# A gated attention layer with a mixture of experts: the residual's scaled normalisation split over VectorE, ScalarE and GpSimd

## Chip, core and metric

One core of a Trainium2 chip. The metric is the device time of one execution in microseconds. Start times in the text are from the profiled span's start.

## What is computed

The first half is an mLSTM attention on 8 sequences of 512 tokens and 256 features, 8 heads, and its output `h` is normalised per token and added to `x`. The second half routes every token to 2 of 9 experts. Cut to what matters:

```python
def _mlstm_cell(q, k, v, ...):                       # q = layernorm(x), k = v = ctx
    C = qk * D_mat                                   # per head, causal
    h = einsum('hst,htd->hsd', C / (normalizer + EPS), vh)
    mu = h.mean(axis=-1, keepdims=True)
    var = h.var(axis=-1, keepdims=True)
    return (h - mu) / sqrt(var + LN_EPS) * ln_scale
x = x + tanh(g_xattn[0]) * _mlstm_cell(...)
x = x + tanh(g_ffn[0]) * experts(layernorm(x))       # top 2 of 9, hidden 704
```

## The kernel before

The program is written by hand: each engine has its own list of instructions, in the order of the code, and semaphores between them. It has three parts. The first (to about 76 us) normalises `x`, transposes it and computes the gates. The second is the attention, in 32 **slots** `t`, one for each tile of 128 tokens (4 tiles `c = t % 4` to a sequence), to about 300 us. The third routes and runs the experts (line 1091 is their matmuls).

In the second part every engine runs one function per slot, `slot_pe`, `slot_act`, `slot_dve`, `slot_pool` and `slot_sync`, and each of them works on several tiles at once: while tile `t` gets its `h`, the decay matrix of tile `t+2` is prepared and tile `t-2` is normalised for the router.

- **VectorE** (`slot_dve`, order of the instructions in a slot): three small steps for the divisor (L620, L622, L624), `h` from PSUM (L627), its statistics (L648) and their mean and variance `mv` (L651), the same for the finished `x2` of tile `t-2` (L657, L660), the state (L610, two instructions; a copy, L605, for one tile in four, nothing for another), `Cm` of tile `t+2` (L587, two), `nb` = minus mean times 1/deviation (L670, 2 columns), and `Cl`, the low bf16 part of `Cm` (L595, two).
- **ScalarE** (`slot_act`): `x2 = h*rs + nb` of tile `t-1` (L677, `c_hn_act`), `y` of `t-3` (L685), the exponentials (L543), `vp` (L555), `yT` (L701), then `lv` and `rs` of tile `t` (L694, L696, `c_rs_act`), which wait for VectorE's L660. Then it waits for GpSimd's last `whl` of the slot before, issues its store (L470, `w_store`), rounds `Cm` to `Ch` (L549, two) and rounds a piece of the experts' weights to bf16 (L464, `w_hi_act`).
- **GpSimd** (`slot_pool`): `kw` (L568) and `qE` (L576), each for three tiles in four, `vp` (L560), then `c_pool` of tile `t-1`: `x2 = x2*lsg` (L712) and `x2 = x2 + xc` (L715), where `lsg` is `tanh(g)*ln_scale` in all partitions and `xc` the residual. Last comes the low part of the weights' piece, in three thirds of 408 columns (L479, `w_pool`), which waits for ScalarE's L464 (semaphore `w_hi`). Slots 0 to 29 have such a piece, slot 13 excepted.
- **TensorE** (`slot_pe`): the products with `Ch` and `Cl` of tile `t`, the scores of tile `t+2`, the decay of `t+3` (L509, L511), the router's products of `t-5` (L729) and a transpose (L721).

`Cm` and `Dm`, `Ch`, `Cl`, `h`, `x2`, `xc` and `lsg` lie in SBUF, `bank` is PSUM. `c_xn` counts ScalarE's finished `x2`, `c_x2` GpSimd's, `c_x2o` the stores to the output.

Of the kernel before, what the change touches and what calls it, by code (L numbers as in the profile page):

```python
# [20 lines left out]
ALU = mybir.AluOpType  # L21
ACT = mybir.ActivationFunctionType
# [10 lines left out]
NC = S // P  # L33
# [27 lines left out]
def build(nc, x, kv, wgate, fib, lnrow, gsc, wroute, rbias, wts, out):  # L61
    with ExitStack() as ctx:
        def sb(name, shape, dt=F32):
            return ctx.enter_context(nc.sbuf_tensor(name, shape, dt))

        def sem(name):
            return ctx.enter_context(nc.semaphore(name))
# [28 lines left out]
        h = sb("h", [P, NC, D])  # L96

        xc = [sb(f"xc{w}", [P, NC, D]) for w in range(2)]; st2 = sb("st2", [P, NC, 6]); st3 = sb("st3", [P, NC, 6])
        mv = sb("mv", [P, NC, 2, 2]); lv = sb("lv", [P, NC, 2]); rs = sb("rs", [P, NC, 2]); nb = sb("nb", [P, NC, 2])
        x2 = sb("x2", [P, NC, D]); y = sb("y", [P, NC, D])  # L100
# [64 lines left out]
        w_in = [sem(f"w_in{w}") for w in range(2)]; w_hi = sem("w_hi"); w_lo = sem("w_lo")  # L165
        w_out = [sem(f"w_out{w}") for w in range(2)]
        c_x = [sem(f"c_x{w}") for w in range(2)]; c_st2 = sem("c_st2"); c_mv2 = sem("c_mv2"); c_st3 = sem("c_st3"); c_mv3 = sem("c_mv3")
        c_nb = sem("c_nb"); c_lv = sem("c_lv"); c_rs = sem("c_rs"); c_xa = sem("c_xa"); c_xn = sem("c_xn"); c_x2 = sem("c_x2"); c_y = sem("c_y"); c_yT = sem("c_yT"); c_yc = sem("c_yc")
        c_lp = sem("c_lp"); c_lg = sem("c_lg"); c_x2o = [sem(f"c_x2o{c}") for c in range(NC)]; c_yo = [sem(f"c_yo{c}") for c in range(NC)]
        s_pace = sem("s_pace")  # L170

        def fence(eng):

            eng.sem_inc(s_pace, 1)

        def ge(eng, sem, val):


            if isinstance(val, int):
                if val > 0:  # L180
                    eng.wait_ge(sem, val)
                return
            eng.wait_ge(sem, val)
            if eng.engine in (nc.sync.engine, nc.gpsimd.engine):
                fence(eng)
# [394 lines left out]
        def b_c_dve(dve, t):  # L580
            for g in range(2):
                ge(dve, b_D, 2 * t + g + 1)
                ge(dve, b_s, t + 1)
                ge(dve, b_Ch, 2 * t + g - 3)
                ge(dve, b_Cl, 2 * t + g - 3)
                by4 = lambda a: a.rearrange("p (j s) -> p j s", j=HG)
                nc.vector.scalar_tensor_tensor(by4(Cm[t % 2][g][:, :]), bank[:, 4:8, g * P:(g + 1) * P], SCALE,  # L587
                                               by4(Dm[t % 2][g][:, :]), ALU.mult, ALU.mult).then_inc(b_C, 1)

        def b_cl_dve(dve, t):  # L590
            ge(dve, b_h, t - 1)
            for g in range(2):
                k = 2 * (t % 2) + g
                ge(dve, b_Ch, 2 * t + g + 1)
                nc.vector.tensor_tensor(Cl[k][:, :], Cm[t % 2][g][:, :], Ch[k][:, :], ALU.subtract).then_inc(b_Cl, 1)  # L595

        def b_st_dve(dve, t):
            V = nc.vector
            b, c = t // NC, t % NC
            if c < NC - 1:  # L600
                ge(dve, b_s, t + 2)
                ub = bank[:, 4:6, UO:UO + HG * DV]
                ge(dve, b_h, t)
                if c == 0:
                    V.tensor_copy(St[0][:, :, :], ub).then_inc(b_st, 1)  # L605
                else:
                    if t == 1:
                        ge(dve, s_dec, 16 * HG)
                    for g in range(2):
                        ins = V.scalar_tensor_tensor(St[c % 2][:, g, :], St[1 - c % 2][:, g, :], dec[:, b, g, c:c + 1],  # L610
                                                     ub[:, g, :], ALU.mult, ALU.add)
                    ins.then_inc(b_st, 1)

        def b_h_dve(dve, t):
            V = nc.vector
            c = t % NC
            ge(dve, b_h, t + 1)
            byg = lambda a: a.rearrange("p (g h) -> p g h", g=2)
            x = hp[:, :, :, DH]
            V.scalar_tensor_tensor(byg(n1[:, :]), x, N_EPS, byg(col[:, t, NH:2 * NH]), ALU.subtract, ALU.max, reverse0=True).then_inc(b_n, 1)  # L620
            ge(dve, b_n, t * 3 + 1)
            V.scalar_tensor_tensor(byg(n2[:, :]), x, N_EPS, byg(n1[:, :]), ALU.add, ALU.max).then_inc(b_n, 1)  # L622
            ge(dve, b_n, t * 3 + 2)
            V.reciprocal(n3[:, :], n2[:, :]).then_inc(b_n, 1)  # L624
            ge(dve, b_n, t * 3 + 3)
            ge(dve, c_xn, t - 3)
            V.tensor_tensor(h[:, c, :].rearrange("p (g h e) -> p g h e", g=2, e=DH), hp[:, :, :, 0:DH],  # L627
                            byg(n3[:, :]).unsqueeze(3).to_broadcast([P, 2, HG, DH]), ALU.mult).then_inc(b_ho, 1)
# [15 lines left out]
        def c_sth_dve(dve, t):  # L644
            V = nc.vector
            c = t % NC
            ge(dve, b_ho, t + 1)
            V.bn_stats(st2[:, c, :], h[:, c, :]).then_inc(c_st2, 1)  # L648
            ge(dve, c_st2, t + 1)
            ge(dve, c_xn, t - 3)  # L650
            V.bn_aggr(mv[:, c, 0, :], st2[:, c, :]).then_inc(c_mv2, 1)  # L651

        def c_stx_dve(dve, t):
            V = nc.vector
            c = t % NC
            ge(dve, c_x2, t + 1)
            V.bn_stats(st3[:, c, :], x2[:, c, :]).then_inc(c_st3, 1)  # L657
            ge(dve, c_st3, t + 1)
            ge(dve, c_y, t - 3)
            V.bn_aggr(mv[:, (c + 2) % NC, 1, :], st3[:, c, :]).then_inc(c_mv3, 1)  # L660

        def c_nb_dve(dve, t):
            r = t % NC
            lo, hi = (0 if t < NT else 1), (2 if t >= 2 else 1)
            ge(dve, c_rs, t + 1)
            ge(dve, c_mv2, min(t + 1, NT))
            ge(dve, c_mv3, t - 1)
            ge(dve, c_xn, t - 3)
            ge(dve, c_y, t - 5)
            nc.vector.scalar_tensor_tensor(nb[:, r, lo:hi], mv[:, r, lo:hi, 0], -1.0, rs[:, r, lo:hi], ALU.mult, ALU.mult).then_inc(c_nb, 1)  # L670

        def c_hn_act(act, t):
            c = t % NC
            ge(act, c_nb, t + 1)
            ge(act, c_y, t - 3)
            ge(act, c_x2o[c], 16 * (t // NC))
            nc.scalar.activation(x2[:, c, :], h[:, c, :], ACT.Identity, bias=nb[:, c, 0:1], scale=rs[:, c, 0:1]).then_inc(c_xn, 1)  # L677

        def c_y_act(act, t):
            c = t % NC  # L680
# [27 lines left out]
        def c_pool(pool, t):  # L708
            G = nc.gpsimd
            b, c = t // NC, t % NC  # L710
            ge(pool, c_xn, t + 1)
            G.tensor_tensor(x2[:, c, :], x2[:, c, :], lsg[:, :], ALU.mult).then_inc(c_xa, 1)  # L712
            ge(pool, c_xa, t + 1)
            ge(pool, c_x[b % 2], 16 * (b // 2) + 16)
            G.tensor_tensor(x2[:, c, :], x2[:, c, :], xc[b % 2][:, c, :], ALU.add).then_inc(c_x2, 1)  # L715

# [29 lines left out]
        def slot_act(act, t):  # L746
            if 0 <= t - 1 < NT:
                c_hn_act(act, t - 1)
            if 0 <= t - 3 < NT:
                c_y_act(act, t - 3)  # L750
            if 1 <= t + 2 < NT:
                b_exp_act(act, t + 2)
            if 1 <= t + 1 < NT:
                b_vh_act(act, t + 1)
            if 0 <= t - 5 < NT:
                c_yc_act(act, t - 5)
            if t >= 9 and (t - 9) % NC == 0:
                c_lg_act(act, (t - 9) // NC)
            if 0 <= t < NT + 2:
                c_rs_act(act, t)  # L760
            if t in PIECE:
                w_store(act, PIECE[t] - 1)
            if t - 1 in PIECE and PIECE[t - 1] == NT - 1:
                w_store(act, NT - 1)
            if 0 <= t + 2 < NT:
                b_ch_act(act, t + 2)
            if t in PIECE:
                w_hi_act(act, PIECE[t])

        def slot_dve(dve, t):  # L770
            if 0 <= t < NT:
                b_h_dve(dve, t)
            if 0 <= t < NT:
                c_sth_dve(dve, t)
            if 0 <= t - 2 < NT:
                c_stx_dve(dve, t - 2)
            if 0 <= t + 1 < NT - 1:
                b_st_dve(dve, t + 1)
            if 0 <= t + 2 < NT:
                b_c_dve(dve, t + 2)  # L780
            if 0 <= t < NT + 2:
                c_nb_dve(dve, t)
            if 0 <= t + 2 < NT:
                b_cl_dve(dve, t + 2)
# [648 lines left out]
```

## Time and profile before

| | |
|---|---|
| time, median of 3 runs | 779.48 us (778.26 to 780.39) |
| profiled execution | 777.09 us |
| its span | 775.3 us |
| PE busy | 663.8 us (86%) |
| DVE busy | 516.8 us (67%) |
| ACT busy | 386.7 us (50%) |
| POOL busy | 409.1 us (53%) |
| mean granted TensorE clock | 0.831 |

PE is TensorE, DVE VectorE, ACT ScalarE and POOL GpSimd. The span runs from the first instruction to the last; the execution's own time is 1.8 us more. The shares are means over three parts with different limits, so those of the second part are read from the trace by stretch. A clock of 1.0 is 2.4 GHz, 0.5 is 1.2 GHz. In a timeline two instructions of a pipelined engine overlap a little: the step from one start to the next is the time that an instruction costs. A row with x2 or x3 holds so many instructions that follow each other.

### The profile page before, as it was taken

To read this page: it belongs to the slowest core of one execution; us is meant where nothing else is said; L and a number is where in the kernel's file an instruction comes from. 1 tells how busy PE (TensorE), PEld (TensorE's weight loads), DVE (VectorE), ACT (ScalarE), POOL (GpSimd) and SP (SyncE) were. 2 spreads that over 40 slices of the span, in tenths; PEclk is the share of its full clock that TensorE was granted. 3 is DMA by queue.
4 is the path that set the end of the run, shared out by engine and by line. 5 is a ranking of instruction groups with operands and counts; after the bars stand their busy time and mean duration, and the time that the engine had idled before them with its cause. 6 is when DMAs were issued, how large, how long until landed. Compare 5 with 4: busy or idle time off the path is not lost.

```text
span 775.3 us, 18373 instructions
## 1 busy us (share of the span) xinstructions
PE 663.8 (86%) x6306; PEld 532.0 (69%) x6306; DVE 516.8 (67%) x1371; ACT 386.7 (50%) x973; POOL 409.1 (53%) x401
## 2 busy tenths in 40 slices
PE   2982989998988953278999999999999999999993
PEld 1541546665665542157889989988989899899893
DVE  7715898999899968945565655565556555555561
ACT  4443677888787761444444433444434344444340
POOL 5025599999999970031454352444443625444423
PEclk9995555556557555579999999999999999999997
DMA  9814789997998851352887797988977968879752
GB/s 282 281 37 125 212 272 272 317 288 241 291 315 277 265 183 30 145 204 94 267 280 251 230 317 204 266 286 245 298 243 230 318 205 274 284 226 301 236 136 47
DMA packets 85820, 179.74 MB, mean 232 GB/s; under 512 B 14881, under 2 KB 48546, under 8 KB 85730
## 3 DMA queue, kind: packets, MB, share of 16 engines
q1 hardware_dynamic: 63202, 140.10, 56.7%
q0 software_dynamic: 13824, 18.43, 11.2%
q10 hardware_dynamic: 8704, 20.06, 6.6%
q8 instruction: 51, 0.84, 0.4%
q14 instruction: 39, 0.32, 0.1%
HBM read 140.93 MB, written 38.67 MB: 232 GB/s over the span
## 4 chain that ended last, share of the span: by engine, by line
PE 54%; POOL 19%; DVE 10%; issue 8%; DMA 4%; ACT 2%; SPq 1%; POOLq 0%; DVEq 0%; ACTq 0%
PE bank L1091 45%; POOL whl L479 8%; DMA out<-res,TS 3%; POOL x L712 3%; POOL vp L560 2%; POOL qE L576 2%; PE bank L298 2%; POOL x L715 2%; PE bank L301 2%; PE bank L1085 1%; POOL kw L568 1%; DVE R L986 1%; PE bank L311 1%; DVE xl L1147 1%; DMA EB<-e_d 1%
## 5 line engine op out<-in xcount | busy, mean ns | idle before, releaser
L1091 PE MATMUL bank<-xh,w 128*128 128x256 bf16 (+1 forms) x1760 | 266.5, 262 | 9.7 <-DVE xl L1147 9.7
L1073 POOL DMA_INDIRECT out<-res,TS x72 | 115.3, 1602 | 213.9 <-DVE res L1208 107.1
L1091 PE MATMUL bank<-xl,w 128*128 128x256 bf16 (+1 forms) x880 | 221.8, 262 | 0.0
L1164 ACT ACTIVATE sg<-bank 128x256 f32<-128x256 f32 (+1 forms) x240 | 86.8, 362 | 228.4 <-PE bank L1091 228.4
L1091 PEld LDWEIGHTS bank<-xh,w 128*128 128x128 bf16 x1760 | 165.0, 98 | 27.9 <-issue 11.9
L1194 DVE TENSOR_TENSOR hf<-sg,bank 128x256 f32<-128x256 f32 (+1 forms) x200 | 78.9, 395 | 115.7 <-ACT sg L1164 115.7
L1091 PE MATMUL bank<-w,hh 128*128 128x256 bf16 x864 | 140.0, 273 | 0.0
L479 POOL TENSOR_TENSOR whl<-wst,whl 128x408 bf16<-128x408 f32 x96 | 94.9, 1015 | 46.7 <-ACT whl L464 46.1
L1064 POOL DMA_INDIRECT xg<-y_d,TG x72 | 72.1, 1002 | 78.9 <-DVE TS L1021 48.4
L1091 PE MATMUL bank<-w,hlo 128*128 128x256 bf16 x360 | 98.1, 273 | 0.0
L1158 ACT CAST hh<-hf 128x256 bf16<-128x256 f32 (+1 forms) x240 | 90.3, 376 | 12.5 <-DVE hf L1196 12.5
L1091 PEld LDWEIGHTS bank<-xl,w 128*128 128x128 bf16 x880 | 86.1, 98 | 8.0
L1091 PEld LDWEIGHTS bank<-w,hh 128*128 128x128 bf16 x864 | 84.5, 98 | 9.3
L1180 DVE TENSOR_TENSOR hlo<-hf,hh 128x256 bf16<-128x256 f32 (+1 forms) x200 | 78.2, 391 | 0.0
L595 DVE TENSOR_TENSOR Cl<-Cm,Ch 128x512 bf16<-128x512 f32 x64 | 67.5, 1091 | 11.3 <-ACT Ch L549 9.1
L1208 DVE TENSOR_SCALAR res<-bank,cws 128x256 f32<-128x256 f32 x72 | 31.8, 479 | 48.6 <-PE bank L1091 48.6
L549 ACT CAST Ch<-Cm 128x512 bf16<-128x512 f32 x64 | 36.8, 617 | 26.5 <-DVE Cm L587 26.5
L509 PE MATMUL bank<-maskb,identb 128*128 128x512 bf16 x64 | 35.5, 554 | 15.3 <-ACT Dm L543 11.0
L587 DVE SCALAR_TENSOR_TENSOR Cm<-bank,Dm 128x512 f32<-128x512 f32 x64 | 41.2, 684 | 7.8 <-ACT Dm L543 7.7
L729 PEld LDWEIGHTS bank<-wr,yT 128*128 128x128 f32 x128 | 27.7, 301 | 20.0 <-ACT yT L701 10.6
L464 ACT CAST whl<-wst 128x1224 bf16<-128x1224 f32 x32 | 38.6, 1209 | 5.3 <-DMA w_d<-whl 5.2
L489 PE MATMUL bank<-qT,kT 32*128 32x128 f32 x512 | 38.7, 445 | 0.0
(218 smaller groups left out, 1058.9 us busy)
## 6 DMA issues: line engine op xcount, KB each, us to landing
w<-w_d SPq DMA_DIRECT2D x40, 1408.0 KB, 9.1
w<-w_d SPq DMA_DIRECT2D x40, 768.0 KB, 4.6
wst<-in_wts SPq DMA_DIRECT2D x32, 612.0 KB, 5.8
w_d<-whl ACTq DMA_DIRECT2D x32, 612.0 KB, 7.2
vb<-in_kv SPq DMA_DIRECT2D x8, 528.0 KB, 5.0
xa<-in_x SPq DMA_DIRECT2D x8, 512.0 KB, 8.3
kT<-in_kv SPq DMA_DIRECT2D x8, 512.0 KB, 8.9
xc<-in_x SPq DMA_DIRECT2D x8, 512.0 KB, 8.1
```

The source lines that it names most:

```text
L464: nc.scalar.copy(whl[w][:, 0, :], wst[w][:, :]).then_inc(w_hi, 1)
L479: ins = nc.gpsimd.tensor_tensor(whl[w][:, 1, cols], wst[w][:, cols], whl[w][:, 0, cols], ALU.subtract)
L489: mm = nc.tensor.matmul(bank[:, 4 + j, g * P:(g + 1) * P], kT[rows, b, c, g * P:(g + 1) * P], qT[rows, b, c, g * P:(g + 1) * P], start=Tru ...
L587: nc.vector.scalar_tensor_tensor(by4(Cm[t % 2][g][:, :]), bank[:, 4:8, g * P:(g + 1) * P], SCALE, by4(Dm[t % 2][g][:, :]), ALU.mult, ALU.m ...
L595: nc.vector.tensor_tensor(Cl[k][:, :], Cm[t % 2][g][:, :], Ch[k][:, :], ALU.subtract).then_inc(b_Cl, 1)
L1064: nc.gpsimd.indirect_dma_start(xg[w][:, j, :], None, y_d, bass.IndirectOffsetOnAxis(ap=TG[:, c0:c0 + 1], axis=0)).then_inc(f_xg[w], 16)
L1073: nc.gpsimd.indirect_dma_start(out, bass.IndirectOffsetOnAxis(ap=TS[:, c0:c0 + 1], axis=0), res[w][:, j, :], None, bounds_check=TOK - 1, o ...
L1091: mm = nc.tensor.matmul(dst, l, r, start=(n == 0), stop=(n == len(pairs) - 1))
L1158: nc.scalar.copy(hh[w][0:K, m, 0:N], hf[m % 3][0:K, 0:N]).then_inc(f_hh, 1)
L1164: nc.scalar.activation(sg[m % 2][0:K, 0:N], bank[0:K, 2 + (NM * w + m) % 4, 0:N], ACT.Silu).then_inc(f_sg, 1)
L1180: V.tensor_tensor(hl_[w][:, m, 0:N], hf[m % 3][:, 0:N], hh[w][:, m, 0:N], ALU.subtract).then_inc(f_hl, 1)
L1194: V.tensor_tensor(hf[m % 3][:, 0:N], sg[m % 2][:, 0:N], bank[:, bk, SLOT:SLOT + N], ALU.mult).then_inc(f_hf, 1)
```

## The change

The scaling by `lsg` moves from the end of the chain (GpSimd) to its start. VectorE makes `(h - mean) * lsg` right after the mean is known (`c_xm_dve`, one instruction with 256 columns, its inputs `h` and `lsg` both in SBUF, the mean a column of `mv`). ScalarE multiplies that by `rs` in place, and no longer needs `nb` for it. GpSimd only adds `xc`. The waits for `c_y` and `c_x2o` move with the first write of `x2` to VectorE. `nb` is still made for `y`.

```diff
+        def c_xm_dve(dve, t):
+            c = t % NC
+            ge(dve, c_mv2, t + 1)
+            ge(dve, c_y, t - 3)
+            ge(dve, c_x2o[c], 16 * (t // NC))
+            nc.vector.scalar_tensor_tensor(x2[:, c, :], h[:, c, :], mv[:, c, 0, 0:1], lsg[:, :], ALU.subtract,
+                                           ALU.mult).then_inc(c_xm, 1)
+
         def c_hn_act(act, t):
             c = t % NC
-            ge(act, c_nb, t + 1)
-            ge(act, c_y, t - 3)
-            ge(act, c_x2o[c], 16 * (t // NC))
-            nc.scalar.activation(x2[:, c, :], h[:, c, :], ACT.Identity, bias=nb[:, c, 0:1], scale=rs[:, c, 0:1]).then_inc(c_xn, 1)
+            ge(act, c_rs, t + 1)
+            ge(act, c_xm, t + 1)
+            nc.scalar.activation(x2[:, c, :], x2[:, c, :], ACT.Copy, scale=rs[:, c, 0:1]).then_inc(c_xn, 1)
...
             ge(pool, c_xn, t + 1)
-            G.tensor_tensor(x2[:, c, :], x2[:, c, :], lsg[:, :], ALU.mult).then_inc(c_xa, 1)
-            ge(pool, c_xa, t + 1)
             ge(pool, c_x[b % 2], 16 * (b // 2) + 16)
             G.tensor_tensor(x2[:, c, :], x2[:, c, :], xc[b % 2][:, c, :], ALU.add).then_inc(c_x2, 1)
...
             if 0 <= t < NT:
                 c_sth_dve(dve, t)
+                c_xm_dve(dve, t)
             if 0 <= t - 2 < NT:
                 c_stx_dve(dve, t - 2)
```

VectorE's list, from `h` to `Cm` in slot 2, which has no state to update (`st` and `mv` are statistics), before:

```order
L627 TENSOR_TENSOR h<-bank,n 128x256
L648 BN_STATS st<-h 128x6
L651 BN_AGGR mv<-st 128x2
L657 BN_STATS st<-x 128x6
L660 BN_AGGR mv<-st 128x2
L587 SCALAR_TENSOR_TENSOR Cm<-bank,Dm 128x512 x2
```

and with the change, with the semaphores that each instruction waits for:

```order
L627 TENSOR_TENSOR h<-bank,n 128x256 [waits b_n]
L648 BN_STATS st<-h 128x6 [waits b_ho]
L651 BN_AGGR mv<-st 128x2 [waits c_st2]
L677 SCALAR_TENSOR_TENSOR x<-h,mv,lsg 128x256 [waits c_mv2]
L657 BN_STATS st<-x 128x6 [waits c_x2]
L660 BN_AGGR mv<-st 128x2 [waits c_st3]
L587 SCALAR_TENSOR_TENSOR Cm<-bank,Dm 128x512 [waits b_Ch,b_Cl,b_s,b_D] x2
```

The new instruction (L677 of the changed file) stands between the mean of `h` and the statistics of the older tile, so L657, L660 and all that follows in the slot come after it.

GpSimd's list in one slot, from `qE` on, before:

```order
L576 TENSOR_TENSOR qE<-qT,EB 128x256
L560 TENSOR_TENSOR vp<-vb,vp 128x264
L712 TENSOR_TENSOR x<-x,lsg 128x256
L715 TENSOR_TENSOR x<-x,xc 128x256
L479 TENSOR_TENSOR whl<-wst,whl 128x408 x3
```

and with the change:

```order
L576 TENSOR_TENSOR qE<-qT,EB 128x256
L560 TENSOR_TENSOR vp<-vb,vp 128x264
L720 TENSOR_TENSOR x<-x,xc 128x256
L479 TENSOR_TENSOR whl<-wst,whl 128x408 x3
L568 TENSOR_TENSOR kw<-vb,col 128x256
```

The multiplication is gone from all 32 slots; the rest keeps its order (L720 is the L715 of before).

## Rows read from the trace of the kernel before

**Rows 1.** The page: the chain that ended last, by engine, whole span.
```profile
PE 54%; POOL 19%; DVE 10%; issue 8%; DMA 4%; ACT 2%; SPq 1%; POOLq 0%; DVEq 0%; ACTq 0%
```

**Rows 2.** Busy us, instructions, TensorE clock, DMA share, GB/s by stretch.
```profile
121.00:279.50 158.50, 142.99 (x1558) 96.34 (x1558) 144.19 (x348) 127.63 (x273) 154.36 (x179) 0.58 0.90 283
121.00:147.50 26.50, 25.57 (x261) 16.84 (x261) 23.86 (x58) 21.28 (x46) 26.19 (x31) 0.50 0.94 290
```

**Rows 3.** VectorE groups, 121 to 279.5 us: busy us, mean ns, idle before.
```profile
L595 DVE TENSOR_TENSOR Cl<-Cm,Ch 128x512 bf16<-128x512 f32 x49 | 53.0, 1120 | 8.6 <-ACT Ch L549 6.9
L587 DVE SCALAR_TENSOR_TENSOR Cm<-bank,Dm 128x512 f32<-128x512 f32 x48 | 30.8, 684 | 0.1
L627 DVE TENSOR_TENSOR h<-bank,n 128x256 f32<-128x256 f32 x25 | 10.6, 424 | 0.9
L670 DVE SCALAR_TENSOR_TENSOR nb<-mv,rs 128x2 f32<-128x2 f32 x24 | 7.5, 311 | 0.0
L610 DVE SCALAR_TENSOR_TENSOR St<-St,dec,bank 128x132 f32<-128x132 f32 x24 | 7.3, 344 | 0.0
```

**Rows 4.** GpSimd groups of the same stretch.
```profile
L479 POOL TENSOR_TENSOR whl<-wst,whl 128x408 bf16<-128x408 f32 x71 | 70.8, 1023 | 2.3 <-ACT whl L464 1.6 <-PE bank L489 0.5
L715 POOL TENSOR_TENSOR x<-x,xc 128x256 f32<-128x256 f32 x24 | 25.0, 1043 | 1.9
```

**Rows 5.** Single lines, the same stretch: ns min/median/max, first and last start.
```profile
L595 DVE TENSOR_TENSOR Cl<-Cm,Ch x49: 686/1183/1219, 120.3 to 277.2; 128x512 bf16<-128x512 f32 x49
L670 DVE SCALAR_TENSOR_TENSOR nb<-mv,rs x24: 150/164/669, 124.8 to 275.2; 128x2 f32<-128x2 f32 x24
L712 POOL TENSOR_TENSOR x<-x,lsg x24: 722/954/1182, 126.0 to 276.0; 128x256 f32<-128x256 f32 x24
```

**Rows 6.** Timeline of one slot: start us, us, engine, line, tile, forms.
```profile
245.02 0.17 DVE L620 SCALAR_TENSOR_TENSOR n<-bank,col 128x8 f32<-128x8 f32 x1
...
245.46 2.79 POOL L479 TENSOR_TENSOR whl<-wst,whl 128x408 bf16<-128x408 f32 x3
...
246.58 0.18 DVE L651 BATCH_NORM_AGGREGATE mv<-st 128x2 f32<-128x6 f32 x1
246.68 0.39 DVE L657 BATCH_NORM_STATS2 st<-x 128x6 f32<-128x256 f32 x1
...
247.10 0.18 DVE L660 BATCH_NORM_AGGREGATE mv<-st 128x2 f32<-128x6 f32 x1
...
247.20 0.60 DVE L610 SCALAR_TENSOR_TENSOR St<-St,dec,bank 128x132 f32<-128x132 f32 x2
...
247.73 1.28 DVE L587 SCALAR_TENSOR_TENSOR Cm<-bank,Dm 128x512 f32<-128x512 f32 x2
...
248.27 0.54 ACTq L470 DMA_DIRECT2D w_d<-whl  x1
...
248.90 0.68 POOL L560 TENSOR_TENSOR vp<-vb,vp 128x264 bf16<-128x264 f32 x1
...
248.93 0.67 DVE L670 SCALAR_TENSOR_TENSOR nb<-mv,rs 128x2 f32<-128x2 f32 x1
...
249.54 0.72 POOL L712 TENSOR_TENSOR x<-x,lsg 128x256 f32<-128x256 f32 x1
249.63 2.32 DVE L595 TENSOR_TENSOR Cl<-Cm,Ch 128x512 bf16<-128x512 f32 x2
...
250.34 1.06 POOL L715 TENSOR_TENSOR x<-x,xc 128x256 f32<-128x256 f32 x1
...
251.37 1.40 POOL L479 TENSOR_TENSOR whl<-wst,whl 128x408 bf16<-128x408 f32 x1
...
251.87 0.15 DVE L620 SCALAR_TENSOR_TENSOR n<-bank,col 128x8 f32<-128x8 f32 x1
```

**Rows 7.** The timeline where GpSimd has nothing to split.
```profile
177.70 1.29 DVE L595 TENSOR_TENSOR Cl<-Cm,Ch 128x512 bf16<-128x512 f32 x2
178.91 0.16 DVE L620 SCALAR_TENSOR_TENSOR n<-bank,col 128x8 f32<-128x8 f32 x1
```

More of the change, by code:

```diff
@@ L167, in build @@
         c_x = [sem(f"c_x{w}") for w in range(2)]; c_st2 = sem("c_st2"); c_mv2 = sem("c_mv2"); c_st3 = sem("c_st3"); c_mv3 = sem("c_mv3")
-        c_nb = sem("c_nb"); c_lv = sem("c_lv"); c_rs = sem("c_rs"); c_xa = sem("c_xa"); c_xn = sem("c_xn"); c_x2 = sem("c_x2"); c_y = sem("c_y"); c_yT = sem("c_yT"); c_yc = sem("c_yc")
+        c_nb = sem("c_nb"); c_lv = sem("c_lv"); c_rs = sem("c_rs"); c_xm = sem("c_xm"); c_xn = sem("c_xn"); c_x2 = sem("c_x2"); c_y = sem("c_y"); c_yT = sem("c_yT"); c_yc = sem("c_yc")
         c_lp = sem("c_lp"); c_lg = sem("c_lg"); c_x2o = [sem(f"c_x2o{c}") for c in range(NC)]; c_yo = [sem(f"c_yo{c}") for c in range(NC)]
```

## The prediction, made before the changed kernel ran

> **What bounds the kernel now.** I read the page's chain first [rows 1]: TensorE has 54% of the span, GpSimd 19%, more than any engine beside TensorE. The change touches the attention part alone, so I took its steady stretch next [rows 2]: in 158.5 us there are 24 slots (24 additions L715, [rows 4]), 6.60 us each. GpSimd is busy for 154.4 us of it, 97%. That is the bound that the chain names. But three others stand close behind. VectorE is busy for 144.2 us, 6.01 a slot. TensorE, at a granted clock of 0.50 (1.2 GHz) in the first 26.5 us, is busy for 25.57 us of four slots, 6.39 a slot. The DMA share is 0.90, at 283 GB/s. So a slot that loses GpSimd work can't become much shorter than 6.4 us while TensorE has the low clock.
>
> VectorE's own rows show what ties it to GpSimd. `Cl` (L595) takes 686 ns at the least and 1183 in the middle, `nb` (L670), 2 columns, 150 to 669 [rows 5]. The timeline shows where the rest comes from [rows 6]: `nb` starts at 248.93 beside `vp` of GpSimd (248.90 to 249.58) and ends at 249.60, just behind it. The first `Cl` starts at 249.63 beside L712 (to 250.26). L715, which starts at 250.34, takes 1.06 us and not the 0.72 of its neighbour, the second `Cl` ends only after L715 has (251.40), and the third of `whl` that starts at 251.37 takes 1.40, against some 0.95 where nothing is in its way. So an instruction of VectorE that reads two operands in SBUF and one of GpSimd go one after the other, whole instructions at a time. `Cm` and `h`, with one operand in PSUM, do not (means of 684 and 424 ns [rows 3]). I call the thing they share the **port**. The Trainium skill has it so (SBUF — State Buffer, the part on who interferes with whom): a VectorE instruction with two SBUF inputs contends with a GpSimd instruction that reads SBUF. The trace agrees, with 1183 ns against 686.
>
> **The change part by part.**
>
> GpSimd loses L712: 0.72 us alone, 0.95 in the middle with its wait for the port [rows 5], 0.80 from its start to that of L715 [rows 6].
>
> VectorE gains one instruction of 256 columns, `xm`. No row has it. Its nearest rows: 424 ns for 256 columns (`h`), 684 for 512 with the constant as a scalar (`Cm`), 344 for 132 with a column as the scalar (`St`) [rows 3]. The first two give (684-424)/256 = 1.02 ns a column; `St` less 132 columns is 210 ns, and 210 + 261 = 0.47 us. The range is 0.42 (as `h`) to 0.55. In the slot, it must also wait for L651's result, 0.18 after that starts, where L657 started 0.10 after it, and the next instruction overlaps it by some 0.08: it adds 0.10 + 0.47 - 0.08 = **0.50 us** to VectorE's slot, before any wait for the port. It has both operands in SBUF, so it does wait, and GpSimd waits for it.
>
> What hides that? VectorE's slot of work without waits: from L620 (245.02) to `nb` (248.93) 3.91, less 0.18 because one slot in four has no L610 and one a shorter copy, `nb` 0.13, and the pair of `Cl` 1.21 where GpSimd does nothing (177.70 to 178.91 [rows 7]): 5.07. The slot is 6.60, so 1.53 us of a slot are waits. Of these, the port has 2 x (1.12 - 0.69) = 0.86 in `Cl` and 0.31 - 0.15 = 0.16 in `nb` [rows 3, 5]. About 0.5 is what comes late from ScalarE, whose `Ch` stands behind the store that waits for GpSimd's `whl` (L470 at 248.27, behind `whl`, 245.46 + 2.79 = 248.25 [rows 6]). With the change VectorE has 5.57 of work, and the question is how much of the 1.53 goes.
>
> I walk one new slot with these steps, VectorE's L620 at 0, for a tile with both L610. The thirds of `whl` begin at 0.12, 1.04 and 1.95 (2.79/3 = 0.93 each). L651 starts at 1.56, `xm` can start at 1.77, waits 0.15 for the second third and ends at about 2.4; the last third is 0.35 later for it, `whl` done at 3.2. L657 starts at 2.31, L660 at 2.73, L610 at 2.83, `Cm` at 3.36 and 3.96. ScalarE has `rs` done at 3.5 and issues the store at once, since `whl` is done: `Ch` at 4.07. `nb` at 4.57 meets `vp` (4.48) and waits 0.42. The first `Cl` finds the port free at 5.11, L715 waits 0.60 for it, the second `Cl` waits 0.55 for L715, and L620 comes again at 6.88. The next three slots, by the same steps, have 6.33, 6.65 and 6.14, since `xm` hardly waits (0.03 to 0.04) and in two of them one `Cl` finds the port free: mean **6.50 us**. The trade is then: 0.50 more work, some 0.35 less port wait (one GpSimd instruction fewer between `vp` and `whl`), some 0.25 less behind ScalarE, because `whl` is no longer the last to finish.
>
> The sum, against the profiled execution (777.09):
> - 26 slots with pieces, (6.50 - 6.60) each: -2.6.
> - About 5 slots where GpSimd holds nobody back (0, 13, 30, 31 and the drain to 300 us): VectorE's 0.50 stands alone: +2.5. At the end L712 (0.72) and the step over `nb` leave the chain of the last tile, -0.2, as the router's transposes bound it anyway.
> - TensorE at the low clock needs 6.39 on average; the slot of 6.14 is too short for it, and what it doesn't catch up in a longer one is lost. Bounds: nothing, and 0.17 a slot (walked with every TensorE step at 1.2 GHz). The low clock holds in most of the stretch (mean 0.58 [rows 2]); I take 0.02 x 24 = +0.5, near nothing because the long slots leave room.
> - ScalarE: the form stays one instruction in place of one, and it waits for `rs` and not `nb`: nothing. It would cost only on ScalarE's queue, which has 0.4 us idle in a slot in the walk. The store's wait `c_x2o` is now VectorE's; that store was issued nearly two slots earlier, so nothing. If a store were late, h's statistics, `Cm` and all TensorE would stand behind it.
>
> Together +0.2, so 777.3 for a profiled execution; the median of the runs stood 2.4 above the profiled one. I forecast **no measurable change, 779.7 us**. A difference under 0.3% (2.3 us) can't be told from none.
>
> **The rivals.**
>
> *GpSimd's time is simply given back (faster).* For it: GpSimd at 97% and its share of the chain. Then the slot falls by what the next bound lets it, to TensorE's 6.39: 26 x -0.21 = -5.5, and +2.3 at the ends: 776.3; with `xm` at 0.42 us the walk gives 6.45, and 779.5 - 0.15 x 26 + 2.0 = 777.6. It would also come about if `xm` did not use the port: the walk without its waits has 6.34. By the skill's sentence above it does use it; the sum without that rule would be 26 x -0.26 + 2.3 = -4.5, 775.0. Chance 0.25.
>
> *`xm` falls behind a third of `whl` that has just begun (slower).* The place is L651's end, 1.77 into the slot. In the walk the second third ends just there. If the slot settles so that the third one starts a tenth of a microsecond ahead of `xm`, `xm` waits 0.85 instead of 0.06, L660, `rs`, the store, `Ch` and the next `whl` move with it, and only the part that `Cl` no longer waits (it would come after L715) comes back, which I put at two thirds. It decides once a third begins between 1.65 and 1.75. The slot is then 6.50 + 0.26 = 6.76, so (6.76 - 6.60) x 26 = +4.2 and the +2.3: 786.0. TensorE at the low clock pushes the same way: with its upper bound the slot is 6.67, and (6.67 - 6.60) x 26 + 2.3 = +4.1, 783.6. Chance 0.25 together.
>
> **How the numbers follow.** No measurable change 0.50, faster 0.25, slower 0.25. The bounds of `xm` (0.42 to 0.55) alone are -1.3 to +2.1 over 26 slots; those of TensorE 0 to +4. From 775.5 to 784.5 the range takes in most of both rivals and leaves out the full wait in each slot.
>
> **What would show it.** Steps right: slots from L620 to L620 of 6.4 to 6.6 us on average, alternating; `xm` between 0.45 and 0.6 us in the middle; GpSimd's busy share under 93%, its idle time in front of `whl`, behind ScalarE's L464; `Cl`'s mean down from 1120 to below 1000 ns; one third of `whl` in three near 1.3 us (mean 1023 ns now [rows 4]). Wrong if `xm`'s mean is over 0.8 us (the slower rival), or if VectorE's idle time grows and TensorE's busy share comes near 1 (its clock), or if slots fall under 6.4.

## The result, and the profile after

The changed kernel takes **785.43 us** (median of 10 runs, 783.28 to 789.82) against 780.36 for the kernel before (10 runs, in part the ones shown above): a ratio of 1.0071, 95% interval 1.0052 to 1.0091. It is slower by 0.7%. The forecast was 779.7 us and no measurable change, the range 775.5 to 784.5; the time lies outside it.

The page after, its span and its chain:

```profile
span 783.7 us, 18405 instructions
...
PE 51%; DVE 9%; DMA 8%; issue 6%; ACT 3%; POOL 3%; ACTq 0%; DVEq 0%; POOLq 0%
```

GpSimd's 19% of the chain [rows 1] is 3% now. The steady stretch, with the columns of [rows 2]:

```profile
121.00:279.50 158.50, 141.76 (x1513) 95.36 (x1513) 147.77 (x358) 121.43 (x265) 128.96 (x152) 0.57 0.87 275
```

GpSimd is busy for 129.0 us where it was for 154.4, VectorE for 147.8 where it was for 144.2. So the work moved as planned, and the engine that seemed to be the bound has 19% of idle time in front of it. The VectorE groups, as in [rows 3] (L677 is the new instruction, called `xm` in the prediction):

```profile
L595 DVE TENSOR_TENSOR Cl<-Cm,Ch 128x512 bf16<-128x512 f32 x46 | 36.9, 842 | 3.4 <-ACT Ch L549 2.8
...
L677 DVE SCALAR_TENSOR_TENSOR x<-h,mv,lsg 128x256 f32<-128x256 f32 x24 | 20.0, 832 | 0.9
...
L657 DVE BATCH_NORM_STATS2 st<-x 128x6 f32<-128x256 f32 x24 | 9.9, 414 | 0.0
L670 DVE SCALAR_TENSOR_TENSOR nb<-mv,rs 128x2 f32<-128x2 f32 x23 | 8.7, 376 | 0.0
```

`Cl` (L595) is down from 1120 to 842 ns. The new instruction takes 832, and its row alone shows that it could take 485:

```profile
L677 DVE SCALAR_TENSOR_TENSOR x<-h,mv,lsg x24: 485/798/1128, 122.0 to 277.6; 128x256 f32<-128x256 f32 x24
L595 DVE TENSOR_TENSOR Cl<-Cm,Ch x46: 677/692/1243, 125.2 to 274.5; 128x512 bf16<-128x512 f32 x46
L670 DVE SCALAR_TENSOR_TENSOR nb<-mv,rs x23: 148/338/746, 124.6 to 273.4; 128x2 f32<-128x2 f32 x23
```

GpSimd's groups, as in [rows 4], and the two waits that stand out in the list of who waited for whom (total us, times, longest):

```profile
L479 POOL TENSOR_TENSOR whl<-wst,whl 128x408 bf16<-128x408 f32 x69 | 68.7, 1023 | 29.7 <-ACT whl L464 29.7
L720 POOL TENSOR_TENSOR x<-x,xc 128x256 f32<-128x256 f32 x23 | 22.0, 957 | 0.0
```

```profile
POOL whl L479 <- ACT whl L464: 29.7, 23, 4.3
...
ACT lv L701 <- issue: 21.8, 24, 2.1
```

GpSimd now waits for ScalarE's L464 before each `whl`, 1.3 us a slot. ScalarE in its turn stands idle ahead of `lv` (L701, the L694 of before), 0.9 us a slot, and `lv` needs VectorE's L660. The profile calls it issue and names no releaser, but one slot shows it (as [rows 6]):

```profile
248.20 3.01 POOL L479 TENSOR_TENSOR whl<-wst,whl 128x408 bf16<-128x408 f32 x3 [0.19 <-ACT whl L464]
...
248.65 0.17 DVE L620 SCALAR_TENSOR_TENSOR n<-bank,col 128x8 f32<-128x8 f32 x1
...
250.21 0.18 DVE L651 BATCH_NORM_AGGREGATE mv<-st 128x2 f32<-128x6 f32 x1
250.43 1.07 DVE L677 SCALAR_TENSOR_TENSOR x<-h,mv,lsg 128x256 f32<-128x256 f32 x1
...
251.18 0.90 POOL L576 TENSOR_TENSOR qE<-qT,EB 128x256 f32<-128x256 f32 x1
...
251.42 0.41 DVE L657 BATCH_NORM_STATS2 st<-x 128x6 f32<-128x256 f32 x1
...
251.86 0.18 DVE L660 BATCH_NORM_AGGREGATE mv<-st 128x2 f32<-128x6 f32 x1
...
252.13 0.30 ACT L701 ACTIVATE lv<-mv,eps_c 128x2 f32<-128x2 f32 x1 [1.48 <-issue]
...
252.52 0.59 ACTq L470 DMA_DIRECT2D w_d<-whl  x1
...
253.26 1.16 ACT L549 CAST Ch<-Cm 128x512 bf16<-128x512 f32 x2 [0.60 <-DVE Cm L587]
...
253.98 1.29 DVE L595 TENSOR_TENSOR Cl<-Cm,Ch 128x512 bf16<-128x512 f32 x2
...
255.38 0.17 DVE L620 SCALAR_TENSOR_TENSOR n<-bank,col 128x8 f32<-128x8 f32 x1
```

L651 ends at 250.39 and the new instruction starts at 250.43 (as recorded; waiting for the port is part of its time). The last third of `whl` has been running since 250.27 or so (248.20 and 3.01 for three thirds), and it ends at 251.2. The new instruction ends only at 251.50, 0.28 us after it. In 29 of the 32 slots a GpSimd instruction holds it up like this, and in each of the 29 it ends 0.28 us after that instruction's end in the trace. It needs 0.485 alone, so its work would run from about 0.2 us before the other's recorded end. It starts 1.76 to 1.78 us into the slot in all 32, so its new waits for `c_y` and `c_x2o` cost nothing here. GpSimd's `qE`, behind it, takes 0.90 and not 0.72. L657 comes at 251.42, L660 at 251.86, 3.21 us into the slot, `lv` at 252.13, the store at 252.52, `Ch` at 253.26, `Cl` at 253.98. `Ch` has a second thing to wait for, `Cm` (L587), which also stands behind the new instruction; the row names it, and in 11 of the 22 steady slots below `Ch` starts 0.09 us after the first `Cm` ends. In the kernel before, the store started 0.04 us after `whl`'s end in 21 of these 22 slots; now it does so in none.

**A slot in three stages.** Everything below is read with one ruler: from the starts in the timeline, a slot is (A) L620 to L660, (B) L660 to the first `Cl`, which contains ScalarE's `lv`, `rs`, store and `Ch`, and (C) `Cl` to the next L620. Means over the same 22 slots of each run's one profile (5 to 29 without 12 to 14, which lie around the slot without `whl`); "31 slots" is from the first L620 to the last.

| kernel | slot | A | B | C | new instr. | 31 slots |
|---|---|---|---|---|---|---|
| before | 6.64 | 2.08 | 2.39 | 2.17 | - | 200.6 |
| after | 6.76 | 3.00 | 2.15 | 1.61 | 0.85 | 206.6 |

A has grown by 0.92: the new instruction's step of 0.5 and its wait. B lost 0.24 and C 0.56, since GpSimd is less in the way. The sum is +0.12, 2.6 us in the 22 slots. The 31 slots took 6.0 us more; 2.2 of that is in slots 12 to 14 (17.9 to 20.1), 0.7 in the last one (5.49 to 6.15) and 0.5 in the first five, where GpSimd has less to give back. The first expert matmul starts at 348.8, only 4.8 us later than before (344.0), because the first slot started 1.3 us earlier (82.0 against 83.2), by a part of the program that the change does not touch: it starts between 82.0 and 83.4 in the runs below. So one profile places a microsecond or so by chance, and that the 4.8 is near the difference of the medians (5.1) is in part luck.

### The profile page after: what moved, and what is told of

Its sections match the earlier page's. It is cut to its first block, busy times and chain, and to the rows that moved or that the text cites. A ratio compares the mean times of both kernels' runs of the same rounds, so it can differ in the third digit from the quotient of the medians.

```text
span 783.7 us, 18405 instructions
## 1 busy us (share of the span) xinstructions
PE 666.0 (85%) x6306; PEld 533.0 (68%) x6306; DVE 527.1 (67%) x1403; ACT 383.3 (49%) x973; POOL 378.9 (48%) x369
## 4 chain that ended last, share of the span: by engine, by line
PE 51%; DVE 9%; DMA 8%; issue 6%; ACT 3%; POOL 3%; ACTq 0%; DVEq 0%; POOLq 0%
PE bank L1097 41%; DMA out<-res,TS 5%; DMA xg<-y_d,TG 2%; PE bank L734 2%; PE bank L1091 2%; PE bank L509 1%; PE bank L511 1%; PE bank L521 1%; DVE Cl L595 1%; DVE R L992 1%; POOL out L1079 1%; PE bank L726 1%; ACT Dm L543 1%; ACT y L692 1%; DMA w_d<-whl 1%
## 5 line engine op out<-in xcount | busy, mean ns | idle before, releaser
L595 DVE TENSOR_TENSOR Cl<-Cm,Ch 128x512 bf16<-128x512 f32 x64 | 49.8, 816 | 4.9 <-ACT Ch L549 3.7
L587 DVE SCALAR_TENSOR_TENSOR Cm<-bank,Dm 128x512 f32<-128x512 f32 x64 | 41.1, 682 | 7.6 <-ACT Dm L543 7.6
L464 ACT CAST whl<-wst 128x1224 bf16<-128x1224 f32 x32 | 38.6, 1208 | 6.0 <-DMA w_d<-whl 6.0
```

## The experiments

Three readings stood against each other. **Port**: the cost is that the new instruction and GpSimd wait for each other. **Work**: it is the 0.5 us of work on VectorE, whatever the port. **Place**: it is what stands behind the instruction, L660 and `Cm`, and through them ScalarE's `Ch` and the next `whl`. All stage numbers are gathered in a table at the end of this section.

### lsg in PSUM, the port taken away

A PSUM bank whose upper half the attention doesn't use holds `lsg`; a wait makes sure that TensorE has finished with that bank in the slot.

```diff
-            nc.vector.tensor_scalar(lsg[:, :], lnr[:, :], tg[:, 0:1], None, ALU.mult).then_inc(s_lsg, 1)
+            nc.vector.tensor_scalar(bank[:, 6, D:2 * D], lnr[:, :], tg[:, 0:1], None, ALU.mult).then_inc(s_lsg, 1)
...
+            ge(dve, b_s, min(t + 3, NT))
...
-            nc.vector.scalar_tensor_tensor(x2[:, c, :], h[:, c, :], mv[:, c, 0, 0:1], lsg[:, :], ALU.subtract,
+            nc.vector.scalar_tensor_tensor(x2[:, c, :], h[:, c, :], mv[:, c, 0, 0:1], bank[:, 6, D:2 * D], ALU.subtract,
```

> The changed kernel with lsg kept in PSUM (the unused half of a bank), so that the new VectorE instruction has only one operand in SBUF. Port theory (it loses its time waiting for a third of whl on GpSimd, and makes the next third late): the instruction takes 0.49 us in every slot, its mean falls from 0.83, slots fall from 6.80 to about 6.45 us, the time to 775 to 778 us. Work theory (VectorE is the bound and its 0.5 us of new work is what counts, not the wait): slots stay above 6.7 us and the time near 784. Clock theory (TensorE at 1.2 GHz is what holds the slots): no change either, 785.

Measured: 778.23 us, ratio to before 0.9973 (0.9952 to 0.9994). Its new instruction:

```profile
L678 DVE SCALAR_TENSOR_TENSOR x<-h,mv,bank x25: 479/481/482, 121.4 to 278.1; 128x256 f32<-128x256 f32 x25
```

The same operation with one operand in PSUM waits in none of its 25 instances. The slot falls from 6.76 to 6.52, somewhat less than expected (6.45), and stage A alone from 3.00 to 2.63. So the wait was real, and worth over 7 us (the ratio goes from 1.0071 to 0.9973). The work theory has fallen in its plain form, the clock too.

One of the 22 slots takes 8.30 us, as ScalarE's L464 at its start waits for a DMA:

```profile
236.36 1.21 ACT L464 CAST whl<-wst 128x1224 bf16<-128x1224 f32 x1 [1.19 <-DMA w_d<-whl]
```

Without that slot the mean is 6.44. Five of the experiments have one or two steady slots of 7.7 to 8.3 us in their profiles, the kernels before and after have none; they lift the mean slot by 0.04 to 0.10.

### GpSimd's multiplication left out, nothing added

This kernel leaves out the scaling by `lsg`, so its result is not the layer's, and the router sees other values.

```diff
-            G.tensor_tensor(x2[:, c, :], x2[:, c, :], lsg[:, :], ALU.mult).then_inc(c_xa, 1)
-            ge(pool, c_xa, t + 1)
```

> The kernel before without GpSimd's multiplication by lsg (left out of the computation), nothing on VectorE: the gain side alone. Port theory: slots of 5.95 to 6.4 us, since VectorE has its old work and one wait for the port less, until TensorE at 1.2 GHz holds them at 6.4: 771 to 775 us. If GpSimd was not what held the slots before (VectorE and the waits behind ScalarE did), slots of 6.5 and 777 to 779.

Measured: 774.62 us, 0.9934 (0.9912 to 0.9955). The slot is 6.34, so only 0.30 us of the 0.95 that L712 took comes back. A stretch of four slots with the clock at 0.50, one of them without a `whl`, the row as in [rows 2]:

```profile
147.50:173.90 26.40, 25.58 (x261) 17.01 (x261) 23.65 (x58) 20.28 (x45) 20.09 (x25) 0.50 0.92 301
```

TensorE is busy for 25.58 of 26.4 us, GpSimd for 20.09. In the kernel before's four slots it was 25.57 of 26.5 us with GpSimd at 26.19 [rows 2]. So with GpSimd's load gone four slots at this clock are no shorter, and TensorE's busy share fits as the reason. No run changes TensorE's work or its clock, so that is not shown. The whole gain that the change could make was 5 us.

### The new instruction added to the kernel before, its result unused

```diff
+            nc.vector.scalar_tensor_tensor(xs[t % 2][:, :], h[:, c, :], mv[:, c, 0, 0:1], lsg[:, :], ALU.subtract,
+                                           ALU.mult).then_inc(c_xm, 1)
```

> The kernel before with the new VectorE instruction added, its result written to a scratch tile and not used: the cost side alone. Port theory: both engines wait for each other more, 0.5 of work, 0.3 of wait on VectorE and 0.37 on GpSimd, partly the same time: slots of 7.1 to 7.3 us, 794 to 800 us. If only GpSimd's delay counts (GpSimd is the bound there, VectorE has 0.5 us of waits to give): slots of 6.97 and about 789.

Measured: 793.60 us, 1.0186 (1.0163 to 1.0209), slots of 7.06, both just under the ranges expected of the port theory. The cost side alone is 14 us, the gain side 5; together they would be +9, and the change costs +5, so 4 us of the two are the same time.

Later the same was run with `lsg` read from PSUM by the added instruction:

> The kernel before with the new instruction added, result unused, but reading lsg from PSUM, so that it needs no port: the cost of its 0.5 us of work alone, where the one with lsg in SBUF gave 7.04 us a slot and 793.6. Port theory: 6.65 to 6.85 us a slot (the work fills waits that VectorE had for GpSimd), 781 to 787. Work theory: 7.0 us and 791 to 794, the port counts for nothing.

Measured: 784.43 us, 1.0068 (1.0048 to 1.0087), slots of 6.70. The work alone costs some 5 us, the port another 9. As expected of the port theory.

### The new instruction behind L657 and L660

```diff
             if 0 <= t < NT:
                 c_sth_dve(dve, t)
-                c_xm_dve(dve, t)
             if 0 <= t - 2 < NT:
                 c_stx_dve(dve, t - 2)
+            if 0 <= t < NT:
+                c_xm_dve(dve, t)
```

> The changed kernel with the new instruction moved behind L657 and L660, so that ScalarE's lv, rs, store and Ch do not wait for it. Port theory: it still meets a third of whl, at another phase (mean 0.7 to 0.9 us); slots of 6.6 to 6.8 us, 780 to 785 us. Theory of the late ScalarE (what costs is that L660 and with it rs, store, Ch and L464 come 0.85 us later, not the wait on VectorE): slots of 6.3 to 6.5 us and 775 to 778.

Measured: 778.91 us, 0.9995 (0.9980 to 1.0010): the kernel before's time. VectorE's groups:

```profile
L595 DVE TENSOR_TENSOR Cl<-Cm,Ch 128x512 bf16<-128x512 f32 x48 | 38.9, 851 | 3.1 <-ACT Ch L549 1.7 <-issue 0.3
...
L677 DVE SCALAR_TENSOR_TENSOR x<-h,mv,lsg 128x256 f32<-128x256 f32 x24 | 19.5, 814 | 0.0
...
L670 DVE SCALAR_TENSOR_TENSOR nb<-mv,rs 128x2 f32<-128x2 f32 x24 | 5.8, 241 | 0.0
```

The new instruction takes 814 ns, hardly less than the 832 in the changed kernel, and `Cl` 851. Its own port wait is all there, and still 6 us are gone (1.0071 to 0.9995). The time and the slots (6.57) lie between the ranges of the two theories. So **what the wait costs depends on where it stands**. One of the slots, which has no L610 and is one of the two steady slots in which the new instruction does not wait:

```profile
252.93 0.17 DVE L620 SCALAR_TENSOR_TENSOR n<-bank,col 128x8 f32<-128x8 f32 x1 [0.72 <-PE bank L535]
...
255.01 0.18 DVE L660 BATCH_NORM_AGGREGATE mv<-st 128x2 f32<-128x6 f32 x1
255.13 0.48 DVE L677 SCALAR_TENSOR_TENSOR x<-h,mv,lsg 128x256 f32<-128x256 f32 x1
255.54 1.27 DVE L587 SCALAR_TENSOR_TENSOR Cm<-bank,Dm 128x512 f32<-128x512 f32 x2
...
257.04 2.08 DVE L595 TENSOR_TENSOR Cl<-Cm,Ch 128x512 bf16<-128x512 f32 x2 [0.16 <-ACT Ch L549]
259.28 0.17 DVE L620 SCALAR_TENSOR_TENSOR n<-bank,col 128x8 f32<-128x8 f32 x1 [0.16 <-PE bank L535]
```

ScalarE in the same slot:

```profile
255.28 0.30 ACT L701 ACTIVATE lv<-mv,eps_c 128x2 f32<-128x2 f32 x1 [0.38 <-issue]
...
255.67 0.56 ACTq L470 DMA_DIRECT2D w_d<-whl  x1
256.32 1.15 ACT L549 CAST Ch<-Cm 128x512 bf16<-128x512 f32 x2 [0.51 <-DVE Cm L587]
```

L660 is 2.08 us into the slot and ScalarE can go on; the new instruction lies beside `lv`, `rs` and the store. Stage A is 2.08 again. B grows from 2.39 to 2.78, by half of the instruction's 0.83: `Cm` still stands behind it, and in 21 of the 22 slots `Ch` now starts 0.09 us after the first `Cm` ends, as here, long after the store's issue is over (0.64 us on average). L620 has TensorE's last product to wait for in this slot (0.16 us).

### The new instruction behind Cm

The same move, further down, ahead of `nb`.

> The changed kernel with the new instruction behind Cm, ahead of nb, lsg in SBUF. There it meets kw, qE and vp of GpSimd (0.61 to 0.72 us each) where it met thirds of whl, and neither L660 nor Cm waits for it. Place theory (it costs what it delays of the chain L660, lv, rs, store, Ch, L464, not its wait alone): slots near those of the kernel with it behind L660 (6.62 us), 777 to 780 us, though its mean stays at 0.75 or more. Port theory alone (its own wait is the cost): slots of 6.7 to 6.8 and 783 to 786.

Measured: **776.27 us**, 0.9967 (0.9949 to 0.9986), faster than both kernels.

```profile
L595 DVE TENSOR_TENSOR Cl<-Cm,Ch 128x512 bf16<-128x512 f32 x48 | 38.4, 839 | 0.4 <-issue 0.3
...
L677 DVE SCALAR_TENSOR_TENSOR x<-h,mv,lsg 128x256 f32<-128x256 f32 x25 | 18.3, 734 | 0.0
L670 DVE SCALAR_TENSOR_TENSOR nb<-mv,rs 128x2 f32<-128x2 f32 x25 | 13.1, 524 | 0.0
```

The waits for the port are (734 - 485) + (524 - 150) + 2 x (839 - 686) = 0.93 us a slot, where the changed kernel has 0.35 + 0.23 + 0.31 = 0.89. As much waiting on VectorE, and 8 us less (1.0071 to 0.9967). The sum of its port waits is no measure of the cost; that the place decides is shown here best. With `Cm` ahead of the instruction too, `Ch` starts 1.51 us after L660, where it was 2.05 with the instruction behind L660; what comes late now is `Cl`, behind `nb`, and ScalarE does not wait for `Cl`. The time (776.27) and the slots (6.49) came below what either theory expected.

### Both repairs together

`lsg` in PSUM and the instruction behind L660.

> Both repairs together: lsg in PSUM, so that the new VectorE instruction needs no port, and the instruction behind L657 and L660. Port theory: the wait (0.33 us a slot in the run with the instruction behind L660) and the place (0.17 us a slot) add up, until TensorE at 1.2 GHz holds the slots at 6.4 us: 773 to 777 us, faster than the kernel before and than either repair alone. If the two repairs give back the same time, or another bound (DMA, TensorE's clock) already holds: 777 to 779, as either alone.

Measured: 776.07 us, 0.9960 (0.9936 to 0.9984), slots of 6.41, the shortest of those that compute the result. Time and slots are in the range of the port theory, but the time is not told apart from that of the run with `lsg` in PSUM alone (0.9973), nor from that of the run before this one (0.9967), which needs no PSUM. From the changed kernel's 6.76 the slot lost 0.35, and 0.24 and 0.19 by either repair alone. Within the pairs, the port is worth 7.6 us with the instruction in its first place (1.0071 to 0.9973) and 2.7 us behind L660 (0.9995 to 0.9960); the place is worth 5.9 us with the port and 1.0 without, which the intervals don't tell from nothing. So the two are not separate costs: it is mainly the wait, at a place where ScalarE stands behind it.

### One instruction for whl, and six

The length of what the new instruction can meet on GpSimd is changed, in the changed kernel.

```diff
-            third = WCH // 3
-            for i in range(3):
+            third = WCH
+            for i in range(1):
```

> The changed kernel with whl written by one instruction of 1224 columns where there are three of 408 (same work). Port theory: a VectorE instruction that meets it waits for the whole of it, up to 2.7 us: the new instruction's mean goes from 0.83 to between 1.3 and 2.0 us, its longest over 2.2, slots to 7.1 to 7.8 us, the time to 793 to 810. If the port were shared in small portions, or the new instruction's length had another cause: mean 0.8 and 783 to 786 us (a little less fixed cost on GpSimd).

Measured: 787.53 us, 1.0098 (1.0064 to 1.0131).

```profile
L677 DVE SCALAR_TENSOR_TENSOR x<-h,mv,lsg x23: 801/1198/2473, 124.6 to 276.6; 128x256 f32<-128x256 f32 x23
L595 DVE TENSOR_TENSOR Cl<-Cm,Ch x46: 677/690/1236, 121.4 to 274.2; 128x512 bf16<-128x512 f32 x46
```

The instruction with 256 columns takes up to 2473 ns and 1304 in the mean; never was it free of a wait in this stretch. The longest:

```profile
206.14 2.50 POOL L479 TENSOR_TENSOR whl<-wst,whl 128x1224 bf16<-128x1224 f32 x1 [3.25 <-ACT whl L464]
...
206.44 2.47 DVE L677 SCALAR_TENSOR_TENSOR x<-h,mv,lsg 128x256 f32<-128x256 f32 x1
```

It arrives 0.3 us into the instruction of 1224 columns and ends 0.28 us after it, as it does beside the ones of 408, so the port is not given up within one. But `Cl` takes 700 ns, nearly free of waits, and the time is 5 us under the range I had expected: what is waited for in stage A is not waited for in C (1.37). The slots are longer than the changed kernel's (6.95 against 6.76), the times are not told apart (1.0064 to 1.0131 against 1.0052 to 1.0091).

With `WCH // 6` and six instructions:

> The changed kernel with whl written by six instructions of 204 columns. Port theory: the new instruction waits at most 0.5 us and about 0.2 on average, its mean falls from 0.83 to about 0.65, slots from 6.79 to 6.6 or 6.7, the time to 780 to 784 us, less what three more fixed costs on GpSimd (which has idle time) take. Otherwise: mean 0.8, time 785 to 788.

Measured: 787.37 us, 1.0094 (1.0063 to 1.0124).

```profile
L677 DVE SCALAR_TENSOR_TENSOR x<-h,mv,lsg x24: 573/680/848, 124.0 to 278.8; 128x256 f32<-128x256 f32 x24
```

```profile
L595 DVE TENSOR_TENSOR Cl<-Cm,Ch 128x512 bf16<-128x512 f32 x48 | 43.1, 937 | 3.6 <-ACT Ch L549 2.2
```

Here the instruction is nearly as short as expected (690 ns in the mean against 650), and `Cl` has the wait back (937 against 842). The steady slots are 6.70, the time no better: 3 us above the range of the port theory and inside that of its rival. The expectation had taken no such return into account. It isn't the only candidate: six pieces also keep GpSimd busy for longer than three (81.7 us for 137 of them, 3.6 a slot, against 68.7 for 69, 3.0 a slot). No run tells the two apart.

### The stages of all runs

| kernel | slot | A | B | C | new instr. | 31 slots | us |
|---|---|---|---|---|---|---|---|
| before | 6.64 | 2.08 | 2.39 | 2.17 | - | 200.6 | 780.36 |
| after | 6.76 | 3.00 | 2.15 | 1.61 | 0.85 | 206.6 | 785.43 |
| lsg in PSUM | 6.52 | 2.63 | 2.18 | 1.72 | 0.48 | 199.9 | 778.23 |
| behind L660 | 6.57 | 2.08 | 2.78 | 1.70 | 0.83 | 201.8 | 778.91 |
| behind Cm | 6.49 | 2.08 | 2.75 | 1.66 | 0.71 | 198.8 | 776.27 |
| PSUM, behind L660 | 6.41 | 2.08 | 2.57 | 1.76 | 0.48 | 197.6 | 776.07 |
| no multiplication | 6.34 | 2.08 | 2.31 | 1.95 | - | 194.7 | 774.62 |
| added to before | 7.06 | 3.14 | 2.23 | 1.69 | 1.00 | 214.3 | 793.60 |
| added, from PSUM | 6.70 | 2.62 | 2.08 | 2.00 | 0.48 | 204.5 | 784.43 |
| whl in one | 6.95 | 3.49 | 2.09 | 1.37 | 1.34 | 211.1 | 787.53 |
| whl in six | 6.70 | 2.82 | 2.15 | 1.72 | 0.69 | 206.4 | 787.37 |

No kernel's B is below 2.08 (no single slot's below 2.01). Its parts in the changed kernel's slot shown above, from L660's start: 0.27 to `lv`, 0.39 from `lv` to the store, 0.74 from the store's issue to `Ch`, 0.72 to `Cl`, 2.12 together; on VectorE's side it is 0.62 to `Cm`, 0.78 from there to `Ch`, and both sides end within 0.1 us of each other. Where the instruction stands in A, B is within 0.15 of this floor in all six such runs, so it has little left to give back for a longer A. Where it stands in B, a part of it lies beside ScalarE's `lv`, `rs` and store. (The times of the table come from four series, in which the kernel before had medians of 780.36, 779.49, 779.68 and 779.04, the first with the result; the ratios in the text are to the one beside them.)

## Why the prediction was wrong

**What bounds the kernel before**: right. GpSimd's 97%, and the others close behind: without L712 the slot falls by 0.30 only (I had said down to 6.39 at the best; it is 6.34), and the time by 5 us; GpSimd's idle time there shows how close the others stood.

**The port**: right, in kind and in size. 479 to 482 ns without it, 485 to 1128 with it, up to 2473 beside a longer instruction. The Trainium skill's rule of two SBUF inputs (SBUF — State Buffer, who interferes with whom) is borne out by the pair of runs that differ in that operand (and in the wait that goes with it), 793.60 and 784.43 us.

**`xm` alone 0.47 us, 0.50 with its place in the queue**: right (0.485; A grows by 0.54 to 0.55 where there is no wait, 2.08 to 2.62 or 2.63).

**The walk, `xm` waits 0.15 in one slot and 0.03 to 0.04 in the next three**: this is the step that failed. The walk gives a mean wait of 0.06; `xm` waits 0.35 in the mean (832 - 485). The trade of a slot had three terms. The work, +0.50, was right. What came late from ScalarE was to fall by 0.25: less work and port waits the slot has some 0.55 before (6.64 - 5.07 - 1.02) and 0.30 after (6.76 - 5.57 - 0.89), so that was right too. The port wait was to fall by 0.35 from before's 1.02; measured it is 0.89, 0.13 less. So the slot grew by 0.12 where it was to shrink by 0.10. The walk had a third of `whl` end at most 0.15 us after `xm` could start (1.77 into the slot, which is what the trace has). In the slot shown the last third begins at about 1.62 (250.27 less 248.65) and has 0.8 us to go when `xm` comes; from slot 18 on the wait repeats with a period of four slots, 0.12, 0.52, 0.30 and 0.58. I had seen that a tenth of a microsecond decides this and made it the slower rival, but the mean of the walk rested on the lucky side.

The wait alone does not mend the walk. For a slot in which `xm` needs no port the prediction has 6.34, and the run with `lsg` in PSUM has 6.52 (6.44 without its one late slot); the port adds 0.24 to that (0.32), where the walk added 0.16. So a part of the walk's shortfall, 0.1 to 0.2, lies in its other steps, and which of them it is stays open; 0.04 is that these 22 slots are 6.64 in the kernel before and not 6.60. The sum's first term was 26 x (6.50 - 6.60) = -2.6; as measured it is 26 x 0.12 = +3.1.

**The slower rival, `xm` behind a third of `whl` that has just begun**: the right mechanism, but the third has been running for a while in most slots, so the wait is 0.35 where I had given it 0.85, and the wrong share is given back. I let two thirds of a wait in A return; from the kernel with `lsg` in PSUM to the changed one A grows by 0.37, B and C give back 0.14, and the slot grows by 0.24. Only a third returns. That the rival's slot of 6.76 and its 786.0 us come so near the measured 6.76 and 785.43 is luck: two errors cancel.

**The slots where GpSimd holds nobody back, +2.5**: near in the sum, 3.3, but not as 0.50 in each of five. Slot 0 has 0.4, slots 12 to 14 have 2.2, slot 30 has 0.7, and from slot 31's start to the first expert matmul it is 0.1.

**TensorE's clock, +0.5**: the stretch has a clock of 0.57 and TensorE is busy for 141.8 of 158.5 us; it has 10% of idle time, more than the 7% that VectorE has, and taking the wait away made the slots 0.24 shorter without it. It was not the cause; whether the clock added anything isn't told apart.

**ScalarE, nothing**: right for the instruction itself (504 ns in place of 597), wrong in what I drew from it: ScalarE's queue is where the delay of L660 and of `Cm` is passed on. The instruction before and after:

```profile
L677 ACT ACTIVATE x<-h,nb,rs 128x256 f32<-128x256 f32 x25 | 14.9, 597 | 0.0
...
L684 ACT ACTIVATE x<-x,rs 128x256 f32<-128x256 f32 x24 | 12.1, 504 | 0.0
```

## What to carry to other kernels

In a ring of engines that hand each other work once a slot, split the slot at the instruction that another engine waits for (here L660, and `Cm` after it). An instruction moved to an engine should stand behind the ones that the busy engines wait for, and not where its data first lie ready: the same instruction, with as much waiting in the slot, cost 5 us ahead of L660 and saved 3 behind `Cm`. And where two engines exclude each other, making one wait shorter can make the next one longer (`whl` in one and in six, 787.5 and 787.4 us), unless an operand is put where the port isn't needed.

## What I had not expected of the hardware

An instruction of VectorE with 256 columns can take 2473 ns, five times its own 485, because of a neighbour on GpSimd; I had expected over 2.2 where `whl` is one instruction, and the least of 23 was 801, so it met GpSimd each time.

The experts' part, whose code no run changes, does not take the same time in all profiled executions: from its first matmul to the end of the span 431.3 us before, 434.9 after, and 440.2 in the run without the multiplication, which had reached that point 7.1 us earlier than before and ended its span at 777.0. Its median is 4.9 us under before's all the same. Which of it is the DMA, the clock at the start of the part, in the run without the multiplication the other values that the router sees, or chance stays open, and so does whether a shorter attention part is given back there.
